# Attention scores in 64x64 tiles of the array, and a cross product's last keys in 32x32 tiles over two banks

## The chip, the core and the metric

One core of a Trainium2 chip runs the whole program in one launch. The metric is the device time of that launch in microseconds. The engines are TensorE (PE in the rows; its weight loads are PEld), VectorE (DVE), ScalarE (ACT), GpSimd (POOL) and SyncE (SP), which issues most DMAs. Each engine works through its own list of instructions in order and waits on semaphores.

## What is computed

Two decoder layers on x of shape (4, 512, 128), with a context of shape (4, 154, 128). The parts that matter here are the first layer's self attention (causal, 16 heads of 8) and its cross attention (16 heads of 8, over 154 context keys):

```python
scores = jnp.einsum('bshd,bthd->bhst', q / jnp.sqrt(Hd).astype(q.dtype), k)
scores = jnp.where(future[None, None, :, :], jnp.finfo(scores.dtype).min, scores)
attn = jax.nn.softmax(scores, axis=-1)
ctx = jnp.einsum('bhst,bthd->bshd', attn, v)
...
scores = jnp.einsum('bhqd,bhkd->bhqk', qh, kh) * scale   # cross: 512 queries, 154 keys
attn = jax.nn.softmax(scores, axis=-1)
out = jnp.einsum('bhqk,bhkd->bhqd', attn, vh)
```

Each is followed by a projection, a residual sum and a layer norm. Then come a gated sum of 8 experts, a linear attention, a second cross attention over the same context with 8 heads, and a gated feed-forward. These five are called "the rest" below.

## The kernel before

**Units.** The self and cross attention of the first layer are done in 32 turns, one for each batch, kind (a = 0 self, a = 1 cross) and group g of four heads. Queries and keys stand in Q6 and K6 as 64 rows for a head (8 features in bf16 parts, and rows that carry the negative maximum), two heads side by side on the partitions: head r of a pair on partitions 64r to 64r+63. A turn has these steps:

- "S" (`scores`, L1117): queries by keys, only to find each query's maximum. Five units u a self turn (SELF_PIECES: two of one piece and three of two), four a cross turn. A unit takes two banks of PSUM, one for each head r. A matmul has 64 rows and 128 columns of weights (L1129), so two of them, r = 0 and 1, lie side by side in the array. In self units the causal mask is added by matmuls of `ident2` with `maskS` (L1136): over 64 columns of each piece (e = 1), then over 128 (e = 0).
- VectorE reduces each unit to maxima (`maxima`, L1820, L1832 to L1837). TensorE transposes them (`max_T`, "mT"), ScalarE copies them, and a DMA on SyncE's queue puts them into Q6 (L804).
- "ST" (`scores_T`, L1141): keys by queries, with the maxima in. Again five self units, of the same widths, with `maskT` (L1158, L1165). A cross turn has two units of 512 queries for the first 128 keys, and one (u = 2) for the last 26 keys, padded to 32, of all four heads in one bank: four matmuls of 64 rows and 32 columns (L1149). ScalarE takes the exponential of each unit into EX (L1570).
- "PV" (`values`, L1170): values by exponentials in f32. A matmul in f32 stands as two records in the trace. Self: 16 matmuls in 128x32 tiles (L1192). Cross: four in 128x32 tiles over 512 queries for the first 128 keys (L1179), then one of the whole array, 128x128 (L1182), for the last keys of the four heads: its weights VXR are block-diagonal, with head j on rows 32j and columns 32j. All into one bank.
- "PV_out": ScalarE copies the bank to `pvraw` (L1474). "cT": TensorE transposes it, and VectorE divides by the sums.

Setup: GpSimd builds `ident2` (L881), the masks and VXR's zeros and ones (L903, L905), and clears Q6[1] in one instruction once the setup products ("wM") are done (L1005). VectorE writes VXR for each batch in `cross_v` (L1918). "wT" are 14 setup transposes of context and weights.

**Order.** It is written out: MERGE is a string of 951 letters, each of which takes the next group of steps from one of 16 streams (`merged`, L363). It sets the order on every engine. BANK_OF names the PSUM bank of each step that fills one; `in_pair` says which steps take the next bank too. A step waits until the earlier users of its banks are drained (`fill`, L1042). Turn (0, self, 0) comes first, then the turns of ORDER; the steps of the rest lie between those of later batches' turns, and the last batch's rest stands alone at the end.

## Time and profile before

| | us |
|---|---|
| median of 3 runs | 489.23 (486.65 to 489.41) |
| the profiled execution | 487.79, of which the span is 486.0 |
| TensorE busy | 459.1 (94%) |
| VectorE busy | 378.0 (78%) |
| ScalarE busy | 344.3 (71%) |
| GpSimd busy | 187.5 (39%) |
| mean granted clock of TensorE | 0.985 of full speed |

A matmul's record runs from its start to its modelled end and overlaps the next one, so the time that a matmul takes from TensorE is read from the distance between starts, not from its own length. In the timeline rows, neighbouring matmuls of one line and form are put together: the first start, the time to the last end, and the count.

### The profile page before, as it was taken

The numbers are of one execution on the slowest core, as the hardware profiler recorded it, in microseconds if no ns is written. First come the engines' busy times: TensorE is split into PE (matmuls) and PEld (weight loads), VectorE is DVE, ScalarE is ACT, GpSimd is POOL, SyncE is SP. The second block draws the span as 40 slices with busy tenths as digits, with TensorE's granted clock in tenths as the row PEclk, the third lists the DMA queues.
The fourth block names the chain that finished last, engine by engine and source line by source line (L and its number), as shares of the span: only waits on it lengthen the run. The fifth ranks groups of instructions, "written<-read, shape, count | busy, mean of one in ns | idle before, by whom it ended". The sixth has DMA issues, their size and how long they took to land.

```text
span 486.0 us, 11581 instructions
## 1 busy us (share of the span) xinstructions
PE 459.1 (94%) x4048; PEld 304.6 (63%) x4048; DVE 378.0 (78%) x1083; ACT 344.3 (71%) x879; POOL 187.5 (39%) x349
## 2 busy tenths in 40 slices
PE   6687899999999999999999999999999999999995
PEld 4454557655455556666777565567764756896895
DVE  4489888798898999995798888847878678765557
ACT  3535758877868788877757787985776868958742
POOL 8590002650204452533233331433414536835423
PEclk9589999999999999999999999999999999999999
DMA  7851300033210211200003000030000000000001
GB/s 229 189 131 36 100 5 25 13 100 82 58 24 1 67 39 35 69 2 0 4 16 93 9 3 2 3 81 13 3 12 14 0 1 2 1 1 1 2 1 43
DMA packets 27181, 18.34 MB, mean 38 GB/s; under 512 B 8217, under 2 KB 26773, under 8 KB 26997
## 3 DMA queue, kind: packets, MB, share of 16 engines
q1 hardware_dynamic: 23413, 15.44, 12.0%
q10 hardware_dynamic: 3712, 2.17, 1.8%
q8 instruction: 33, 0.54, 0.5%
q14 instruction: 23, 0.19, 0.1%
HBM read 5.58 MB, written 1.05 MB: 14 GB/s over the span
## 4 chain that ended last, share of the span: by engine, by line
PE 38%; POOL 5%; DVE 4%; ACT 3%; issue 3%; SPq 1%; DMA 1%; POOLq 0%; DVEq 0%; ACTq 0%
PE psum L1066 5%; PE psum L1425 4%; PE psum L1436 4%; PE psum L1402 3%; PE psum L1338 3%; PE psum L1129 2%; PE psum L1158 2%; PE psum L1192 2%; PE psum L1182 2%; PE psum L1179 2%; SPq L797 1%; PE psum L1447 1%; POOL GP L1024 1%; POOL rstd_rest L955 1%; ACT REST L1653 1%
## 5 line engine op out<-in xcount | busy, mean ns | idle before, releaser
L1570 ACT ACTIVATE EX<-psum 128x1024 f32<-128x1024 f32 (+1 forms) x128 | 118.1, 979 | 12.9 <-PE psum L1165 8.3
L1837 DVE TENSOR_REDUCE mparts<-psum 128x2 f32<-128x768 f32 (+1 forms) x96 | 77.5, 861 | 4.8 <-PE psum L1136 4.5
L1832 DVE TENSOR_REDUCE mparts<-psum 128x4 f32<-128x616 f32 (+1 forms) x80 | 67.8, 875 | 4.7 <-PE psum L1129 4.0
L1129 PE MATMUL psum<-K,Q 64*128 64x154 bf16 (+4 forms) x512 | 47.4, 268 | 5.6 <-issue 2.1
L1024 POOL TENSOR_TENSOR GP<-REST,xrs 128x512 f32<-128x512 f32 (+1 forms) x48 | 33.1, 713 | 46.6 <-DVE xrs L2066 32.6
L1158 PE MATMUL psum<-Q,K 64*128 64x512 bf16 (+3 forms) x320 | 41.4, 315 | 3.6 <-DMA Q<-mrows 1.8
L1653 ACT ACTIVATE REST<-psum,nxmax 128x154 f32<-128x154 f32 x96 | 36.2, 396 | 10.1 <-DVE nxmax L2056 7.9
L1474 ACT COPY pvraw<-psum 128x512 f32<-128x512 f32 x32 | 18.7, 584 | 32.4 <-PE psum L1192 23.4
L1192 PE MATMUL psum<-EX,V 128*32 128x256 f32 (+3 forms) x512 | 37.7, 435 | 0.0
L1129 PEld LDWEIGHTS psum<-K,Q 64*128 64x128 bf16 x512 | 19.0, 95 | 28.9 <-issue 18.4
L952 POOL TENSOR_SCALAR rstd_rest<-moments_rest 128x2 f32<-128x2 f32 x32 | 7.3, 228 | 74.9 <-DVE moments_rest L1872 74.4
L952 POOL TENSOR_SCALAR rstd_attn<-moments_attn 128x4 f32<-128x4 f32 x8 | 1.9, 238 | 83.9 <-DVE moments_attn L1872 83.8
L2056 DVE TENSOR_REDUCE nxmax<-psum 128x2 f32<-128x308 f32 x64 | 28.8, 469 | 5.6 <-PE psum L1402 5.2
L1402 PE MATMUL psum<-GP,xT 128*128 128x308 f32 x96 | 30.5, 433 | 0.1
L1192 PEld LDWEIGHTS psum<-EX,V 128*32 128x32 f32 x512 | 14.6, 109 | 18.4 <-issue 16.9
L1136 PE MATMUL psum<-maskS,ident 64*128 64x128 bf16 (+2 forms) x320 | 24.7, 232 | 0.0
L1698 ACT ACTIVATE X<-Y_rest,shift_rest,rstd_rest 128x128 f32<-128x128 f32 x36 | 15.9, 493 | 11.8 <-POOL shift_rest L960 11.7
L1425 PE MATMUL psum<-VM,REST 128*128 128x128 f32 x192 | 23.8, 277 | 0.2 <-DVE VX L1928 0.2
L955 POOL TENSOR_TENSOR rstd_rest<-rstd_rest,power 128x2 f32<-128x2 f32 x32 | 22.9, 716 | 2.7
L1165 PE MATMUL psum<-maskT,ident 64*128 64x128 bf16 (+2 forms) x320 | 23.8, 227 | 0.0
L1425 PEld LDWEIGHTS psum<-VM,REST 128*128 128x128 f32 x192 | 22.6, 192 | 1.3 <-issue 0.7
L1158 PEld LDWEIGHTS psum<-Q,K 64*128 64x128 bf16 x320 | 13.0, 94 | 15.9 <-issue 6.8
(343 smaller groups left out, 1150.2 us busy)
## 6 DMA issues: line engine op xcount, KB each, us to landing
Q<-xparts SPq DMA_DIRECT2D x24, 128.0 KB
Q<-parts SPq DMA_DIRECT2D x21, 128.0 KB
K<-parts SPq DMA_DIRECT2D x21, 128.0 KB
X<-in_x SPq DMA_DIRECT2D x4, 256.0 KB, 3.1
Q<-in_L_xattn_Wkv SPq DMA_DIRECT2D x1, 1024.0 KB, 7.2
K<-xkparts SPq DMA_DIRECT2D x24, 38.5 KB
out<-XB_rest SPq DMA_DIRECT2D x6, 128.0 KB, 1.8
Q<-in_L_xattn_Wq SPq DMA_DIRECT2D x1, 512.0 KB, 4.3
```

The costliest lines, as they stand in the source:

```text
L955: return nc.gpsimd.tensor_tensor(to, to, half_power, ALU.pow)
L1024: last = nc.gpsimd.tensor_tensor(of.XP[:, at:at + 4 * n].rearrange("p (h c) -> p h c", h=4)[:, :, 0:c1 - c0], of.XE[:, :, c0:c1], of.xrs.r ...
L1129: last = mm(to[:, r, at:at + n], Q6[a][p, b % 2, 2 * g + jj, P * q:P * q + P], K6[a][p, b % 2, 2 * g + jj, 0:n], start=at == 0 or bool(a), ...
L1158: last = mm(to[:, r, at:at + n], K6[a][p, b % 2, 2 * g + jj, P * k:P * k + P], Q6[a][p, b % 2, 2 * g + jj, P * k:S], start=at == 0 or bool ...
L1192: last = mm(to[32 * h:32 * h + 32, P * k:S], V[:, k, 4 * g + h, :], EX[:, ex_slot(b, a, g, u) + h % 2, at:at + n], start=k == PV_ORDER[0], ...
L1402: fills_(mm(fill(key)[:, 0:2 * C], half_of(b, h).xT[4][:, P * q:P * q + P], G[:, head:head + 2, :].rearrange("p h c -> p (h c)")), key)
L1425: mm(to, of.XPT[:, head, :], VM[:, head, :], start=head == 0, stop=False)
L1570: drains(nc.scalar.activation(dst, src, ACT.Exp), key)
L1653: last = nc.scalar.activation(of.XE[:, i, :], src[:, C * j:C * j + C], ACT.Exp, bias=of.nxmax[:, i:i + 1], accum_out=of.xsum[:, i:i + 1])
L1832: last = vec.tensor_reduce(nmax[:, :, :, q], src[:, :, 0:2 * n].rearrange("p r (j k) -> p r j k", j=2), AX.X, ALU.max, negate=True)
L1837: last = vec.tensor_reduce(nmax[:, :, jj, q], src[:, :, at:at + P * (q + 1)], AX.X, ALU.max, negate=True)
L2056: vec.tensor_reduce(of.nxmax[:, 2 * side:2 * side + 2], src, AX.X, ALU.max, negate=True).then_inc(xmax_ready[z], 1)
```

## The change

- **S and ST in 64x64 tiles.** Each matmul of 64 rows and 128 columns becomes two of 64 rows and 64 columns, e = 0 and 1, which write partitions 0 to 63 and 64 to 127 of the same bank. In self units the half e that needs fewer keys (S) or queries (ST) gets 64 fewer. The mask is four matmuls a unit as before, but each has 64 rows of output: S adds 128 columns of mask to half 0 and 64 to half 1; ST 64 and 128. `ident2` shrinks to 64 columns. Matmuls of L1129 and L1158 double, from 512 to 1024 and from 320 to 640.
- **The last cross keys.** ST's unit u = 2 becomes eight matmuls of 256 queries: in the second half of the queries, head h stands on partitions of head h + 2 (modulo 4). PV for cross takes a pair of banks, one for each half of the queries: eight matmuls in 128x32 tiles over 256 queries each, then eight in 32x32 tiles, with rows 32h in the first half and 32(h + 2) in the second. VXR holds every head's 32 columns at all four row groups, so `cross_v` writes 128 columns in each of its four parts instead of 32. ScalarE copies the two half banks in one instruction.
- **The clear** of Q6[1] on GpSimd is eight memsets of 512 words, the last of which signals.
- **New tables** MERGE and BANK_OF of the same lengths; MERGE has each letter as often as before.

What the tables say, when they are followed step by step: in both, turn (0, cross, 0) begins at about the 172nd of 1031 steps and turn (3, cross, 0) at the 692nd. Before the first S unit, the old one has one "wT" (n = 0) and the new one nine (n = 0 to 8), four of them ahead of "qkT". Counted over TensorE's order, neighbouring pieces of work differ in the shape of their tiles 265 times with the old tables and tiles, and 302 times with the new. Of the 16 cross PV steps, 12 are followed in the old order by work of the whole array. In the core of the diff, the rows of the tables after the first are left out:

```diff
--- before.py
+++ after.py
@@ -327,36 +327,38 @@
-    return step[1] in ("S", "ST") and not (step[1] == "ST" and step[2] and step[4] == 2)
+    _, what, *at = step
+    return (what == "S" or what == "ST" and not (at[0] and at[2] == 2)
+            or what == "PV" and at[0] == 1)
...
 MERGE = (
-    "rrrrrrrrlwrrlllwrrrurrsssssuuuvuuuuussssstttrsrttslssspptssttttpsslsrppsttststtupllu"
...
+    "rrrrrruuuurrlrwrlllwuururrrruusssssvusrsssttsstrltstsslspptssttttpsssrplptststtstplu"
...
 BANK_OF = (
-    "024613570246124602454675401724062402640724062460240672460246042604523605260426402367"
...
+    "714325431736704126510425310562402642050362406246024067246702640260452604260426402367"
@@ -464,7 +466,7 @@
-            zeros = VXR[CR:32, :, :].rearrange("p g c -> p (g c)").bitcast(BF16)
+            zeros = VXR[CR:32, :, :].rearrange("p h c -> p (h c)").bitcast(BF16)
             return (Q6[a][MAX_ROWS, b % 2, :, :].rearrange("p (o j) t -> p o (j t)", o=4),
@@ -494,7 +496,7 @@
-        ident2 = sb("ident2", [P, 2, P], BF16)
+        ident2 = sb("ident2", [P, TILE], BF16)
         maskS = sb("maskS", [P, 2, P], BF16)
@@ -541,7 +543,7 @@
         VX = sb("VX", [P, H, 32])
-        VXR = sb("VXR", [P, NQ, P])
+        VXR = sb("VXR", [P, H, 32])
         mparts = sb("mparts", [P, 2, 80])
@@ -878,8 +880,8 @@
                 p = slice(TILE * r, TILE * r + TILE)
-                nc.gpsimd.affine_select(out=ident2[p, :, :], in_=ones_of[p, :, :],
-                                        pattern=[[TILE, 2], [-1, P]], compare_op=ALU.is_equal,
+                nc.gpsimd.affine_select(out=ident2[p, :], in_=ones_of[p, 0, 0:TILE],
+                                        pattern=[[-1, TILE]], compare_op=ALU.is_equal,
                                         fill=0.0, base=0, channel_multiplier=1)
@@ -903,7 +905,7 @@
                     step(nc.gpsimd.memset(
-                        VXR[32 * j:32 * j + CR, :, 32 * j + HD:32 * j + HD + 1], 1.0))
+                        VXR[32 * j:32 * j + CR, :, HD:HD + 1], 1.0))
                 nc.gpsimd.memset(vaug[:, :, :], 1.0).then_inc(late_zeros_ready, 1)
@@ -1002,8 +1004,10 @@
                     pool.wait_ge(bank_filled[k], m + 1)
-                    nc.gpsimd.memset(words(Q6[1].rearrange("p b h t -> p (b h) t")), 0.0
-                                     ).then_inc(cross_rows_ready, 1)
+                    zeroed = words(Q6[1].rearrange("p b h t -> p (b h) t"))
+                    for i in range(8):
+                        last = nc.gpsimd.memset(zeroed[:, S * i:S * i + S], 0.0)
+                    last.then_inc(cross_rows_ready, 1)
                     step(nc.gpsimd.memset(XP, 0.0))
@@ -1114,6 +1118,22 @@
+            def in_tiles():
+
+                for e in R:
+                    for r in R:
+                        yield e, r, *[slice(TILE * i, TILE * i + TILE) for i in (e, r)]
+
+            def mask(to, starts, of, cols_of):
+
+                for e, r, half, p in in_tiles():
+                    cols = cols_of[e]
+                    last = mm(diagonals(to[half, r, :], starts, cols), ident2[p, :],
+                              of[p, e:e + 1, cols].to_broadcast(
+                                  [TILE, len(starts), cols.stop - cols.start]),
+                              start=False, stop=True, skip_group_check=True)
+                return last
+
             def scores(b, a, g, u):
@@ -1123,19 +1143,16 @@
                 for at, jj, q in PIECES[a][u]:
-                    n = C if a else P * (q + 1)
-                    for r in R:
-                        p = slice(TILE * r, TILE * r + TILE)
-                        last = mm(to[:, r, at:at + n], Q6[a][p, b % 2, 2 * g + jj, P * q:P * q + P],
-                                  K6[a][p, b % 2, 2 * g + jj, 0:n], start=at == 0 or bool(a), stop=bool(a))
-                for e in (() if a else (1, 0)):
-
-                    cols = slice(TILE * e, P)
-                    for r in R:
-                        p = slice(TILE * r, TILE * r + TILE)
-                        last = mm(diagonals(to[:, r, :], [at + P * q for at, _, q in PIECES[a][u]], cols),
-                                  ident2[p, e, :], maskS[p, e:e + 1, cols].to_broadcast([TILE, len(PIECES[a][u]), cols.stop - cols.start]),
-                                  start=False, stop=e == 0)
+                    for e, r, half, p in in_tiles():
+
+                        n = C if a else P * q + TILE * (e + 1)
+                        last = mm(to[half, r, at:at + n],
+                                  Q6[a][p, b % 2, 2 * g + jj, P * q + TILE * e:P * q + TILE * e + TILE],
+                                  K6[a][p, b % 2, 2 * g + jj, 0:n], start=bool(a) or at == 0,
+                                  stop=bool(a), skip_group_check=not a)
+                if not a:
+                    last = mask(to, [at + P * q for at, _, q in PIECES[0][u]], maskS,
+                                [slice(0, P), slice(TILE, P)])
                 fills_(last, key)
@@ -1144,28 +1161,33 @@
                 if a and u == 2:
-                    for h in range(4):
+                    for n, h, rest, cols in rests():
                         p = slice(TILE * (h % 2), TILE * (h % 2) + TILE)
-                        last = mm(to[32 * h:32 * h + 32, :], K6[1][p, b % 2, 2 * g + h // 2, P:CP],
-                                  Q6[1][p, b % 2, 2 * g + h // 2, :], start=True, stop=True)
+                        last = mm(to[rest, cols], K6[1][p, b % 2, 2 * g + h // 2, P:CP],
+                                  Q6[1][p, b % 2, 2 * g + h // 2, cols], start=True, stop=True,
+                                  skip_group_check=True)
                     fills_(last, key)
...
                 for at, jj, k in ([(0, u, 0)] if a else SELF_T_PIECES[u]):
-                    n = S - P * k
-                    for r in R:
-                        p = slice(TILE * r, TILE * r + TILE)
-                        last = mm(to[:, r, at:at + n], K6[a][p, b % 2, 2 * g + jj, P * k:P * k + P],
-                                  Q6[a][p, b % 2, 2 * g + jj, P * k:S], start=at == 0 or bool(a), stop=bool(a))
-                for e in (() if a else R):
-
-                    cols = slice(0, TILE * e + TILE)
-                    for r in R:
-                        p = slice(TILE * r, TILE * r + TILE)
-                        last = mm(diagonals(to[:, r, :], [at for at, _, _ in SELF_T_PIECES[u]], cols),
-                                  ident2[p, e, :], maskT[p, e:e + 1, cols].to_broadcast([TILE, len(SELF_T_PIECES[u]), cols.stop - cols.start]),
-                                  start=False, stop=e == 1)
+                    for e, r, half, p in in_tiles():
+
+                        q = P * k + (0 if a else TILE * e)
+                        last = mm(to[half, r, at + q - P * k:at + S - P * k],
+                                  K6[a][p, b % 2, 2 * g + jj, P * k + TILE * e:P * k + TILE * e + TILE],
+                                  Q6[a][p, b % 2, 2 * g + jj, q:S], start=at == 0, stop=bool(a),
+                                  skip_group_check=not a)
+                if not a:
+                    last = mask(to, [at for at, _, _ in SELF_T_PIECES[u]], maskT,
+                                [slice(0, TILE), slice(0, P)])
                 fills_(last, key)
+
+            def rests():
+
+                for n in HALVES:
+                    for h in range(4):
+                        at = 32 * ((h + 2 * n) % 4)
+                        yield n, h, slice(at, at + 32), slice(HS * n, HS * n + HS)
@@ -1175,12 +1197,17 @@
                         drained(pe, (b, "xv"))
-                    for h in range(4):
-                        mm(to[32 * h:32 * h + 32, :], VX[:, 4 * g + h, :],
-                           EX[:, ex_slot(b, a, g, h // 2) + h % 2, :],
-                           start=True, stop=False, skip_group_check=True)
-                    fills_(mm(to, VXR[:, g, :], EX[:, ex_slot(b, a, g, 2), :], start=False, stop=True,
-                              skip_group_check=True), key)
+                    to = pair(key)
+                    for n in HALVES:
+                        for h in range(4):
+                            mm(to[32 * h:32 * h + 32, n, 0:HS], VX[:, 4 * g + h, :],
+                               EX[:, ex_slot(b, a, g, h // 2) + h % 2, HS * n:HS * n + HS],
+                               start=True, stop=False, skip_group_check=True)
+                    for n, h, rest, cols in rests():
+                        last = mm(to[32 * h:32 * h + 32, n, 0:HS], VXR[rest, 4 * g + h, :],
+                                  EX[rest, ex_slot(b, a, g, 2), cols], start=False, stop=True,
+                                  skip_group_check=True)
+                    fills_(last, key)
                     return
@@ -1476,6 +1503,9 @@
+            def halved(t):
+                return t.rearrange("p (n t) -> p n t", n=2)
+
             def place_first(b, y, w):
@@ -1577,6 +1607,12 @@
                 drains(copy(mrows[:, parity(b, a, g), :], src[0:48, 0:64].bitcast(BF16)), key)
+
+            def products_out(b, a, g):
+                key = (b, "PV", a, g)
+                filled(act, key)
+                drains(copy(halved(pvraw[:, :]), pair(key)[:, :, 0:HS]) if a else
+                       copy(pvraw[:, :], bank(key)), key)
@@ -1706,7 +1742,7 @@
                     "ST": exponentials, "mT": max_T,
-                    "PV_out": lambda b, a, g: move(pvraw[:, :], (b, "PV", a, g)),
+                    "PV_out": products_out,
                     "ctxT": lambda b, a: move(ctxT[:, :], (b, "ctxT", a)),
@@ -1921,10 +1957,8 @@
                     vec.tensor_tensor(
-                        VXR[at, :, 32 * j:32 * j + HD],
-                        src[at, P:2 * P].rearrange("p (g h d) -> p g h d", g=NQ, h=4)[:, :, j, :],
-                        rows[at, BV, :].rearrange("p (g h d) -> p g h d", g=NQ, h=4)[:, :, j, :],
-                        ALU.add)
+                        VXR[at, :, 0:HD], src[at, P:2 * P].rearrange("p (h d) -> p h d", d=HD),
+                        rows[at, BV, :].rearrange("p (h d) -> p h d", d=HD), ALU.add)
                 drains(vec.tensor_tensor(VX[:, :, 0:HD],
...
```

## Rows read from the trace of the kernel before

**Rows 1.** Stretches: length, busy (count) of PE, PEld, DVE, ACT, POOL; clock, DMA

```profile
0.00:60.00 60.00, 45.06 (x425) 28.69 (x426) 42.70 (x101) 29.92 (x50) 28.22 (x49) 0.89 0.51 136
...
60.00:220.00 160.00, 156.60 (x1643) 93.22 (x1641) 142.21 (x364) 123.45 (x255) 52.46 (x86) 1.00 0.16 40
...
220.00:380.00 160.00, 158.74 (x1345) 103.28 (x1344) 124.16 (x370) 119.42 (x314) 55.73 (x116) 1.00 0.08 19
...
380.00:486.00 106.00, 98.66 (x642) 79.41 (x640) 68.93 (x250) 71.54 (x262) 51.14 (x99) 0.99 0.02 6
...
27.00:60.00 33.00, 28.90 (x375) 17.72 (x376) 30.47 (x49) 19.33 (x30) 9.13 (x13) 0.95 0.30 80
```

**Rows 2.** Timeline, matmuls of three self units: start, us, form, count

```profile
158.21 0.39 PE L1129 MATMUL psum<-K,Q 64*128 64x512 bf16 x2
...
158.52 0.38 PE L1129 MATMUL psum<-K,Q 64*128 64x512 bf16 x2
...
158.91 0.65 PE L1307 MATMUL psum<-mv,cT 128*32 128x128 f32 x16
...
139.55 0.39 PE L1129 MATMUL psum<-K,Q 64*128 64x256 bf16 x4
...
139.94 0.38 PE L1158 MATMUL psum<-Q,K 64*128 64x512 bf16 x2
...
140.16 0.25 PE L1165 MATMUL psum<-maskT,ident 64*128 64x64 bf16 x4
```

**Rows 3.** Timeline, a cross unit, a cross product and what follows it

```profile
202.95 0.31 PE L1129 MATMUL psum<-K,Q 64*128 64x154 bf16 x4
...
203.19 1.06 PE L1179 MATMUL psum<-EX,VX 128*32 128x512 f32 x8
...
204.18 1.13 PE L1182 MATMUL psum<-EX,VXR 128*128 128x512 f32 x2
...
205.15 0.60 PE L1066 MATMUL psum<-ident,X 128*128 128x128 f32 x4
```

**Rows 4.** Timeline, another cross product, followed by a score unit

```profile
138.49 1.13 PE L1182 MATMUL psum<-EX,VXR 128*128 128x512 f32 x2
```

**Rows 5.** Groups by line and form: count, busy us, mean ns

```profile
L1149 PE MATMUL psum<-Q,K 64*32 64x512 bf16 x64 | 6.3, 387 | 0.0
...
L1129 PEld LDWEIGHTS psum<-K,Q 64*128 64x128 bf16 x512 | 19.0, 95 | 28.9 <-issue 18.4 <-ACT EX L1570 2.9 <-DMA Q<-xparts 1.7
...
L1192 PEld LDWEIGHTS psum<-EX,V 128*32 128x32 f32 x512 | 14.6, 109 | 18.4 <-issue 16.9 <-ACT EX L1570 0.9
...
L1182 PEld LDWEIGHTS psum<-EX,VXR 128*128 128x128 f32 x32 | 4.8, 188 | 13.4 <-issue 13.4
...
L1201 PEld LDWEIGHTS psum<-identb,mparts 128*80 128x80 bf16 x32 | 3.7, 117 | 2.4 <-issue 2.0
```

**Rows 6.** Stretches again, for L1136 alone, then for L1182 alone

```profile
60.00:220.00 160.00, 12.73 (x172) 7.71 (x172) 1.00 0.16 40
...
220.00:380.00 160.00, 5.13 (x68) 3.05 (x68) 1.00 0.08 19
...
60.00:220.00 160.00, 6.75 (x12) 1.78 (x12) 1.00 0.16 40
```

**Rows 7.** Waits: us in total, times, longest us

```profile
ACT pvraw L1474 <- PE psum L1182: 9.0, 7, 2.6
```

**Rows 8.** Timeline of the start, with the setup transposes

```profile
14.85 1.97 PE L1066 MATMUL psum<-ident,qkn 128*128 128x128 f32 x8 [5.37 <-DVE qkn L1770]
...
27.10 0.39 PE L1129 MATMUL psum<-K,Q 64*128 64x512 bf16 x2 [2.08 <-issue]
...
32.53 1.64 PE L1066 MATMUL psum<-ident,Q 128*128 128x128 f32 x13
```

**Rows 9.** Groups by line: two memsets of GpSimd

```profile
L1005 POOL MEMSET Q<- 128x4096 f32 x1 | 3.5, 3512 | 4.4 <-PE psum L1253 4.4
...
L903 POOL MEMSET VXR<- 128x512 f32 x1 | 0.5, 524 | 0.1
```

40 lines of the change are left out of this document (20 added, 20 removed).

## The prediction

> **What bounds the kernel now.** I read the busy time by stretches first. From 60 to 380 us TensorE is busy 98 to 99% of the time, VectorE 89% up to 220 us and 78% after it, and the granted clock is 1.00, the 2.4 GHz level [rows 1]. But a busy TensorE may be one that waits with overlapping records, so I read the timeline next, by distances between starts. A self unit of S with one piece takes 158.52 - 158.21 = 0.31 us. Its two matmuls side by side have 512 columns, its masks 64 and 128: 704 columns at 2.4 GHz are 0.293 us, and four steps of some 3 ns make it 0.31. A unit with two pieces (256 + 256, masks of 128 and 256: 896 columns, 0.373 us) takes 139.94 - 139.55 = 0.39 us, and 512 columns alone take 140.16 - 139.94 = 0.22 us [rows 2]. So in such runs TensorE is bound by the columns that stream through it: columns that are taken away there are time. The same one-piece unit, followed by work in another shape of tiles, takes 158.91 - 158.52 = 0.39 us: a change of shape costs 0.08 to 0.09 us [rows 2]. The start is another matter: from 27 to 60 us VectorE is busy 30.5 of 33 us and TensorE 28.9 [rows 1]. After 380 us there is only the rest, where TensorE is busy 98.7 of 106 us [rows 1] and which the change does not touch.
>
> **Self units in four tiles.** With the halves e side by side, a one-piece unit streams 448 + 128 columns in one half and 512 + 64 in the other: 576 / 2.4 = 0.240 us, with the steps 0.25. A two-piece unit streams at most 640: 0.267 us, with the steps 0.28. ST is the mirror image. Against 0.31 and 0.39 that saves 0.06 and 0.11 us. Matmuls start in the order of the list, so one half sometimes waits for the other; I take 0.01 off each. A turn has two and three such units in S, and again in ST: 2 x 0.05 + 3 x 0.10 = 0.40 us a side, and 32 sides make 12.8 us.
>
> **Does the array do it?** No row shows 64x64 tiles. The nearest is 64x32: 64 matmuls of 387 ns are busy 6.3 us, that is 0.39 us for each four, so four tiles in two row groups run at once, each with its own stream [rows 5]. In 128x32 tiles, 16 matmuls of 128 columns in f32 take 0.65 us [rows 2], four at a time. From above: if halves ran at once at no cost, 12.8 us plus the 1.6 that I took off. From below: one after the other, which is a rival below. I take the near end.
>
> **Weight loads.** A load of 64x128 in bf16 takes 95 ns, one of 80 columns 117 ns; in f32, 32 columns take 109 ns and 128 take 188 ns, 0.82 ns a column [rows 5]. A load starts when the tile's previous matmul starts, so only its streaming part can hold the next one. At 0.82 ns, 64 columns take 53 ns, as long as a mask of 128 columns streams; only a mask of 64 columns (27 ns) is shorter. So the cost lies between nothing and 0.026 us x 160 units = 4.2 us. I take nothing: the extra 22 ns of the 80-column load over the 128-column one is less than what a mask of 64 columns streams. The Trainium skill speaks against the change here ("TensorEngine Tiling (Array Packing)", Restrictions and Gotchas): column tiling switches off the fast weight load, which the 64x128 loads have and the 64x64 ones would not. By that rule the sum would be up to 4.2 us worse; the trace agrees so far that the 80-column bf16 load is the longer one.
>
> **Cross units.** S: four matmuls of 154 columns two at a time become eight, four at a time: the same 0.13 us of streaming (a unit takes 203.19 - 202.95 = 0.24 us with the change of shape [rows 3]), and 0.01 us for the longer row of starts, 64 times: -0.6 us. ST's units of 512 queries stay at 0.22 us; the last keys' eight matmuls of 256 columns are two on each of four tiles, as long as four of 512: nothing.
>
> **Cross products.** The first part takes 204.18 - 203.19 = 0.99 us [rows 3]; four rounds of 256 columns for two of 512 leave it. The second takes 205.15 - 204.18 = 0.97 us where work of the whole array follows [rows 3], and 139.55 - 138.49 = 1.06 us where a score unit does [rows 4, 2]. Its two records are 2 x 512 / 1.2 = 0.853 us (f32 streams at half rate), the rest is the first weight load. After: eight tiles, all different, so two records of 256 columns: 0.427 us; a load of 32 columns for 128, 0.03; eight starts, 0.05; a change of shape behind it, always, 0.09: 0.60 us. Twelve products save 0.37 and four 0.46: 6.3 us. If the two halves ran one after the other it would be 16 x 0.43 = 6.9 us less, none; I take the near end, as eight tiles share nothing. ScalarE copies the same 512 columns as before.
>
> **New tables.** Changes of shape go from 265 to 302. Twelve of these 37 are in the products' 0.60; the other 25 cost 25 x 0.09 = 2.3 us. Eight more setup transposes come ahead of the first score. TensorE idles 5.4 us before 14.85 and 2.1 before 27.10, and five of the eight show later as 13 records in 1.64 us and more of the kind [rows 8]; nothing is lost by them if their loads have landed, and what they free lies in 27 to 60 us, where VectorE is the bound. Bounds: 0 and some 6 us (eight at up to 0.87 us, the time of eight records 0.11 us apart).
>
> **Other edits.** `cross_v` writes wider pieces on VectorE, a few tenths of a us over four batches. The clear: 4096 words take 3.5 us, 512 take 0.52, so eight take at most 4.2 [rows 9]; 0.7 us more on GpSimd, busy 52 of 160 us there [rows 1], hides under the work of TensorE; without that cover it would be 0.7 us. A smaller `ident2` is ahead of the scores by 20 us: nothing.
>
> **The sum.** 12.8 + 6.3 - 0.6 - 2.3 = 16.2 us of TensorE. Where do they fall? Of 320 mask matmuls in S, 172 run in 60 to 220 us and 68 after, which leaves 80 before 60 us; of the 32 records of the whole-array product 12 run in 60 to 220 us [rows 6].
> - To 60 us: 3.2 us of self units. VectorE leaves 33 - 30.5 = 2.5 us; I take 2.0, with whatever the moved transposes give.
> - 60 to 220 us: 6.9 + 2.4 - 1.6 (costs by share) = 7.7 us. VectorE would then be busy 142.2 of 152.3 us, 93%, and each engine waits for the others through eight banks. I take two thirds: 5.1.
> - 220 to 380 us: 2.7 + 3.9 - 1.3 = 5.3 us, with VectorE at 124 of 155: all of it.
> - After 380 us: nothing.
>
> Together 12.4 us. The profiled execution took 487.8 us, 1.8 outside its span; 487.8 - 12.4 = 475.4. The median stands 1.4 us higher, which gives 476.8. I take 476.
>
> **Rivals.**
> 1. *Starts come no closer than they do now.* The densest run in the rows is 15 starts in 0.65 - 0.28 = 0.37 us, 25 ns each [rows 2]. If that is a floor, a cross unit of eight needs 0.20 us and not 0.13 (64 x 0.065 = 4.2 us) and a two-piece unit of twelve 0.30 and not 0.28 (96 x 0.02 = 1.9). 482 us. For it: no denser run; against: neighbours in one round start a few ns apart. The skill's "TensorE: Matmul & The Clock Gate" (Wait — 56ns, not 53.3ns?) has such a floor, about 25 ns from start to start however few the columns; the starts inside a round are closer than it says. Chance 12%.
> 2. *VectorE becomes the bound* up to 220 us. Only the last stretch gains, 5.3 us: 484 us. For it: 89 and 92% busy; against: TensorE was 98% busy beside it. 16%.
> 3. *Weight loads bind* by 4.2 us: 480 us. 4%.
> 4. *Slower: the pair for cross products.* They need two neighbouring banks free where one did, while score units take pairs too, and all that TensorE has behind them (score units that VectorE and ScalarE wait for) waits along. ScalarE waited up to 2.6 us for such a product [rows 7], so delays of this size exist. Each us that one product waits costs 16; above 12.4 / 16 = 0.78 us each the gain is gone. At 1.1 us it is 494 us. Against: the order was written anew with the pairs in it. 10%, of which 4% stay within 1%.
> 5. *Slower: halves do not run at once.* One-piece units would take 0.48 us, two-piece 0.53, and the cross ones 0.13 and 0.21 more: 32 x (2 x 0.17 + 3 x 0.14) + 64 x 0.13 + 32 x 0.21 = 39 us, less 6.3: about 522 us. It costs more than it gains when less than about two thirds of the halves overlap. 6%.
>
> **Numbers.** The forecast has 52%. About 1%, 5 us, is what a measurement of this kernel can tell from no change. Faster by more: 52 + 12 + 4 + 7 of rival 2 = 75%. Within: 9 of rival 2 and 4 of rival 4, 13%. Slower: 12%. The range: down to 489 - 16.2 - 6 = 467 if all of TensorE's gain and all of the moved transposes count, up to 486, past rivals 1 to 3. The forecast's own range is 469 to 481.
>
> **What would show it.** Distances between starts of units: 0.25 and 0.28 us for self units, about 0.60 us from the first 32x32 matmul to the next work; cross units at 0.13 us before the change of shape. TensorE's busy time some 12 to 15 us lower, at an unchanged tail of about 106 us; VectorE above 91% from 60 us on. It is wrong if units take 0.30 us and more, if TensorE shows idle time ahead of the cross products, or if VectorE waits longer than before for S units.

## The result, and the profile after

The changed kernel takes 484.94 us (median of 20 runs, 484.05 to 488.91), the kernel before 487.78 us beside it (20 runs, 486.53 to 490.68): a ratio of 0.994, 95% interval 0.9924 to 0.9956. It is faster by 2.8 us, 0.6%, within the 1% that I called no change; I had forecast 12 us. The profiled execution has a span of 484.8 us against 486.0.

The stretches of the changed kernel, in the columns of [rows 1], show that the matmuls were not what failed:

```profile
27.00:60.00 33.00, 27.48 (x477) 15.31 (x481) 31.08 (x53) 19.07 (x27) 9.62 (x12) 0.80 0.31 80
60.00:220.00 160.00, 152.17 (x2203) 90.20 (x2193) 143.79 (x357) 120.22 (x245) 53.21 (x95) 0.98 0.16 42
...
220.00:380.00 160.00, 158.67 (x1922) 105.99 (x1922) 128.39 (x380) 123.21 (x325) 55.13 (x116) 1.00 0.07 18
```

From 60 to 220 us TensorE is busy 152.2 us where it was 156.6, and VectorE 143.8 against 142.2: TensorE has got idle time, and VectorE is hardly busier for it. The granted clock, 1.00 there before, is 0.98, and from 27 to 60 us 0.80 in place of 0.95.

The timeline of the changed kernel (start, us, form, count) answers to [rows 2 to 4]: S units at 133.90 (one piece) and 136.20 (two), a cross product at 134.61 and 135.61, an ST unit of two pieces at 141.48.

```profile
133.90 0.41 PE L1149 MATMUL psum<-K,Q 64*64 64x448 bf16 x4
...
134.16 0.34 PE L1149 MATMUL psum<-K,Q 64*64 64x320 bf16 x6
...
134.61 1.07 PE L1203 MATMUL psum<-EX,VX 128*32 128x256 f32 x16
135.61 0.66 PE L1207 MATMUL psum<-EX,VXR 32*32 32x256 f32 x16
136.20 0.36 PE L1149 MATMUL psum<-K,Q 64*64 64x320 bf16 x6
...
136.50 0.38 PE L1176 MATMUL psum<-Q,K 64*64 64x512 bf16 x4
...
141.48 0.38 PE L1176 MATMUL psum<-Q,K 64*64 64x128 bf16 x8
...
141.76 0.38 PE L1176 MATMUL psum<-Q,K 64*64 64x128 bf16 x8
```

From start to start: one piece 134.16 - 133.90 = 0.26 us (0.31 before), two pieces 136.50 - 136.20 = 0.30 and 141.76 - 141.48 = 0.28 us (0.39 before), the first part of the product 1.00 us (0.99), the second 136.20 - 135.61 = 0.59 us (0.97 to 1.06). Not every unit saves as much. The medians of all self units of ST after 60 us are 0.27 us (one piece) and 0.30 us (two) where another score unit follows, for 0.31 and 0.39 before; where the shape of the tiles changes behind them they are 0.37 and 0.40 us, for 0.40 and 0.49.

Where the time went can be read off one instruction of VectorE that ends the maxima of each of the 32 turns. Timelines, six of the 32, the kernel before and then the changed one:

```profile
59.76 0.17 DVE L1847 TENSOR_TENSOR mparts<-mparts 128x16 f32<-128x16 f32 x1
...
102.98 0.17 DVE L1847 TENSOR_TENSOR mparts<-mparts 128x16 f32<-128x16 f32 x1
...
152.88 0.17 DVE L1847 TENSOR_TENSOR mparts<-mparts 128x16 f32<-128x16 f32 x1
...
181.84 0.17 DVE L1847 TENSOR_TENSOR mparts<-mparts 128x16 f32<-128x16 f32 x1
...
225.21 0.17 DVE L1847 TENSOR_TENSOR mparts<-mparts 128x16 f32<-128x16 f32 x1
...
366.37 0.17 DVE L1847 TENSOR_TENSOR mparts<-mparts 128x16 f32<-128x16 f32 x1
```

```profile
58.90 0.17 DVE L1883 TENSOR_TENSOR mparts<-mparts 128x16 f32<-128x16 f32 x1
...
100.19 0.17 DVE L1883 TENSOR_TENSOR mparts<-mparts 128x16 f32<-128x16 f32 x1
...
150.22 0.17 DVE L1883 TENSOR_TENSOR mparts<-mparts 128x16 f32<-128x16 f32 x1
...
183.30 0.28 DVE L1883 TENSOR_TENSOR mparts<-mparts 128x16 f32<-128x16 f32 x1
...
227.13 0.17 DVE L1883 TENSOR_TENSOR mparts<-mparts 128x16 f32<-128x16 f32 x1
...
365.09 0.18 DVE L1883 TENSOR_TENSOR mparts<-mparts 128x16 f32<-128x16 f32 x1
```

The changed kernel is 0.9 us ahead at 59 us, 2.8 at 100, 2.7 at 150; then 1.5 us behind at 182 and 1.9 at 225; and 1.3 ahead at 366, and 1.2 at the end. So there are two things to explain: 4.2 us lost at one place between 150 and 183 us, and gains that are small everywhere else.

To size them I added up TensorE's records. A record streams its columns at 2.4 GHz (512 columns of bf16 in 0.22 us) or, in f32, at 1.2 GHz (256 columns in 0.215 us, the distance of two rounds in the product at 134.61). The rest is half clock (what the same columns take longer while the granted clock is at its 1.2 GHz level), changes of shape (idle time where the shape changes, up to 93 ns each) and waits:

```
us                         waits   streaming  half clock  changes (count)
before                      50.2     396.4       7.9       25.9 (284)
tiles alone, old tables     57.7     385.7      10.4       25.9
tables alone                52.6     396.9       8.1       28.0 (306)
changed                     56.4     380.2      14.0       28.6 (315)
changed, addition held      55.6     380.2      10.8       28.6
held, both readers light    50.0     380.6       6.5       28.6
```

16.2 us of streaming are gone and 2.7 us of changes of shape have come, 13.5 us net; 6.2 us came back as waits and 6.1 us as stretches at 1.2 GHz. The other rows are from runs below. The rows leave out some 5.6 us of the span, and how overlapping records are divided between the columns is a choice: another division moves a column by up to 6 us, but the differences between the rows by no more than 0.6.

### The profile page after: what moved, and what is told of

The parts are those of the page before. It is cut to its first block, busy times and chain, and to the rows that moved or that the text cites. A ratio compares the mean times of both kernels' runs of the same rounds, so it can differ in the third digit from the quotient of the medians.

```text
span 484.8 us, 14106 instructions
## 1 busy us (share of the span) xinstructions
PE 454.0 (94%) x5296; PEld 304.7 (63%) x5296; DVE 383.4 (79%) x1083; ACT 346.0 (71%) x879; POOL 187.7 (39%) x356
## 4 chain that ended last, share of the span: by engine, by line
PE 72%; DVE 11%; ACT 5%; SPq 4%; issue 3%; POOL 2%; DMA 2%; POOLq 0%; DVEq 0%; ACTq 0%
PE psum L1070 10%; PE psum L1452 6%; PE psum L1219 6%; PE psum L1429 6%; PE psum L1365 6%; PE psum L1149 5%; DVE mparts L1873 4%; PE psum L1176 4%; PE psum L1463 4%; PE psum L1203 3%; PE psum L1474 2%; SPq L771 2%; PE psum L1207 2%; DMA K<-parts 2%; PE psum L1247 2%
## 5 line engine op out<-in xcount | busy, mean ns | idle before, releaser
L1149 PE MATMUL psum<-K,Q 64*64 64x154 bf16 (+8 forms) x1024 | 51.2, 274 | 8.4 <-DVE mparts L1873 2.7
L1176 PE MATMUL psum<-Q,K 64*64 64x512 bf16 (+7 forms) x640 | 43.3, 320 | 3.2 <-ACT EX L1600 1.1
L1149 PEld LDWEIGHTS psum<-K,Q 64*64 64x64 bf16 x1024 | 22.7, 108 | 34.5 <-issue 15.7
L1176 PEld LDWEIGHTS psum<-Q,K 64*64 64x64 bf16 x640 | 16.2, 108 | 19.6 <-issue 7.7
L1365 PE MATMUL psum<-ew,xT 128*128 128x512 f32 x48 | 24.8, 656 | 0.0
L1615 ACT COPY pvraw<-psum 128x512 f32<-128x512 f32 x16 | 9.4, 584 | 20.5 <-PE psum L1219 20.5
L1131 PE MATMUL psum<-maskS,ident 64*64 64x128 bf16 (+2 forms) x320 | 22.3, 241 | 0.0
L933 POOL COPY V<-qkn 128x256 f32<-128x256 f32 x8 | 3.7, 467 | 44.8 <-PE psum L1219 44.7
```

Source lines behind the costliest of these rows:

```text
L1149: last = mm(to[half, r, at:at + n], Q6[a][p, b % 2, 2 * g + jj, P * q + TILE * e:P * q + TILE * e + TILE], K6[a][p, b % 2, 2 * g + jj, 0:n ...
L1176: last = mm(to[half, r, at + q - P * k:at + S - P * k], K6[a][p, b % 2, 2 * g + jj, P * k + TILE * e:P * k + TILE * e + TILE], Q6[a][p, b ...
L1365: fills_(mm(fill(key), half_of(b, h).xT[2][:, P * i:P * i + P], ew[:, 4 * side:4 * side + 4, :].rearrange("p e d -> p (e d)")), key)
```

## Experiments

Each was timed beside the kernel before; the number given is the ratio to it with its 95% interval. A difference of two such ratios is uncertain by 1.6 to 2.1 us.

### The parts one by one

**Tiles alone, old tables.** The kernel before with the score units in 64x64 tiles and nothing else:

```diff
...
-                        last = mm(to[:, r, at:at + n], Q6[a][p, b % 2, 2 * g + jj, P * q:P * q + P],
...
+                    for e, r, half, p in in_tiles():
...
+                        last = mm(to[half, r, at:at + n],
+                                  Q6[a][p, b % 2, 2 * g + jj, P * q + TILE * e:P * q + TILE * e + TILE],
...
```

> The kernel before with its own MERGE and BANK_OF, its own cross product and its one-piece clear; only the score units S and ST run in 64x64 tiles. By the sum, TensorE streams some 12 us less. Theory A (the array was the bound only in part: what it is spared comes back as waits for VectorE and ScalarE and as stretches at the 1.2 GHz level, whatever the order): about 4 to 5 us faster than before, ratio about 0.991, with more wait and more half-clock time in the trace. Theory B (the new tables bring the waits and the clock drops): 9 to 11 us faster, ratio about 0.98, and faster than the changed kernel, with the clock as high as in before.

**Tables alone.** The new `MERGE` and `BANK_OF` with the pair of banks for the cross product and the clear in eight pieces; the score tiles and the product are those of before, and ST's last keys run as eight matmuls of 256 queries in place of four of 512:

> The new MERGE and BANK_OF (the cross product holds two banks and fills one) and the eight-piece clear, with the score tiles and the cross product of before. Streamed columns as before. Theory A: within 2 us of before. Theory B: 5 to 9 us slower than before, with drops of the clock after 27 us that before does not have.

**Tiles on the new tables**, with the product of before:

> The changed kernel with the cross product of before (VXR block-diagonal, one 128x128 matmul for the last keys, one bank filled of the two held). Against the changed kernel TensorE streams 6.3 us more. Theory A: 2 to 4 us slower than the changed kernel, about level with before. Theory B: the product is full profit wherever it stands, so 6 us slower than the changed kernel, some 3 us slower than before. If the pair of banks were what costs (rival 4), this kernel would have the same waits ahead of the products and not be slower by more than its 6 us of streaming.

**Product on the new tables**, with the score units of before:

> The changed kernel with the 64x128 score tiles of before. Against the changed kernel TensorE streams some 12 us more. Theory A: 3 to 6 us slower than the changed kernel, so level with or up to 3 us slower than before, with less wait and less time at the lower clock than the changed kernel. Theory B: 10 us or more slower than the changed kernel, about 1.5% slower than before.

Measured: tiles on the old tables 0.9972 (0.995 to 0.9994), tables alone 1.0089 (1.0064 to 1.0114), tiles on the new tables 1.0027 (1.0006 to 1.0049), product on them 1.0001 (0.998 to 1.0023). So the new tables cost 4.3 us by themselves; on them the tiles are worth 3.0 us and the product 4.3, and both together 7.3 (1.0089 to 0.994): they add up. On the old tables the tiles are worth 1.4 us, although the sum of records gives 10.7 us less streaming. What is missing there is no cost of the tiles themselves but something that takes the gain. The eight-piece clear is in all kernels with the new tables and was not timed by itself.

### Is it VectorE? Is it the clock at the start?

**Fewer columns for the maxima**, for the kernel before and for it with the tiles (`[:, :, :, 0:n // 2]` on what the two kinds of `tensor_reduce` read; these kernels leave out half of the keys in the maxima and serve for the time alone):

> The kernel before, but VectorE's maxima of the first layer's scores read the first half of each piece's keys only, so some 60 to 70 us of VectorE's 378 us are gone; TensorE's work is unchanged. The maxima are then not those of all keys. If TensorE alone bounded the kernel: within 1 us of before. If VectorE sets the pace up to 220 us (rival 2 of the prediction): 3 to 6 us faster than before.

> The same lighter maxima with the 64x64 score tiles and the old tables (e1). What the tiles are worth with VectorE out of the way is this kernel against e6. Theory of rival 2 (VectorE took the gain): 8 to 11 us faster than e6. Theory E (the gain is lost elsewhere: ScalarE's exponentials, latencies from engine to engine, the clock): 1 to 3 us faster than e6, as e1 is against before.

Measured: 0.9955 (0.9933 to 0.9978) without the tiles and 0.9954 (0.9924 to 0.9984) with them. With VectorE light the tiles are worth nothing on the old tables (0.0 us, give or take 1.8), so VectorE alone is not what takes the gain there. Idle time of TensorE's weight loads for S from 60 to 380 us, without and with tiles (after the bar: busy; idle, and what ended it):

```profile
L1129 PEld LDWEIGHTS psum<-K,Q 64*128 64x128 bf16 x446 | 15.7, 94 | 21.9 <-issue 15.0 <-ACT EX L1570 2.1 <-DMA Q<-xparts 1.1
```

```profile
L1145 PEld LDWEIGHTS psum<-K,Q 64*64 64x64 bf16 x896 | 18.6, 106 | 28.1 <-issue 15.8 <-DMA K<-parts 3.2 <-ACT EX L1580 3.1
```

With tiles there are twice as many loads and the idle time before them is 6.2 us longer; no VectorE is among its first releasers: ScalarE's exponentials (1.0 us more) and a transfer of keys (3.2) are.

**Dummy matmuls at the start**, four ahead of each of the first ten S units, to hold the clock up:

> The kernel with 64x64 score tiles and the old tables (e1), with four matmuls of 128 columns in f32 (about 0.9 us at 2.4 GHz) put ahead of each of the ten S units of the first batch's first two turns, into the unit's own bank; they compute nothing that is kept. In e1 the clock stood at 1.2 GHz until 37.8 us (30.9 in before) and the second turn's scores were done 2.7 us later than in before. Theory C (the low clock at the start costs e1 its gain): the clock is up by about 31 us, the second turn's scores are done at about 42 us, and the kernel is 2 us faster than e1, ratio about 0.993 to before. Theory D (VectorE sets the pace there, and the clock is a symptom): no faster than e1, 0 to 3 us slower.

Measured: 1.0154 (1.0121 to 1.0186). From 27 to 60 us the granted clock was 0.95 instead of 0.84, and yet the second turn's maxima ended at 50.84 us instead of 44.35. The dummies took more of TensorE than the clock gave back. That does not say which engine bounds the start without them, for with them VectorE is busy only 22.7 of the 33 us. The runs with light maxima say more. The stretch from 27 to 60 us, tiles on the old tables, then the same with light maxima:

```profile
27.00:60.00 33.00, 27.86 (x467) 17.42 (x467) 28.25 (x46) 18.41 (x28) 9.12 (x12) 0.84 0.26 69
```

```profile
27.00:60.00 33.00, 26.56 (x491) 16.90 (x491) 21.10 (x54) 20.71 (x32) 9.17 (x12) 0.95 0.30 78
```

With less for VectorE to read, the clock is at 0.95 with no dummy at all, and the instruction that ends the fourth turn's maxima starts at 57.57 us instead of 61.74. In the kernel before it starts at 57.25 with light maxima and at 59.76 without. So VectorE does hold up the start, as I had it in the prediction; what I had left out is that TensorE's clock goes down with it.

### Both readers of the score banks

A score unit needs two banks, and they are free once VectorE (maxima) or ScalarE (exponentials) has read them. If that sets the pace, the tiles pay when both read less. Beside the light maxima, ScalarE's exponentials leave out half of each bank from the second batch on:

```diff
...
+                elif b:
+                    dst, src = EX[:, slot_:slot_ + 2, 0:S // 2], pair(key)[:, :, 0:S // 2]
                 else:
                     dst, src = flat(EX[:, slot_:slot_ + 2, :]), flat(pair(key))
...
```

> The kernel before with two kinds of work cut in half: both of VectorE's kinds of row maxima read half of their columns (as in the run of the kernel before with light maxima), and from the second batch on ScalarE's exponentials of a two-bank unit read and write only the first 256 of 512 columns of each bank. The rest of EX keeps older numbers, so this is a kernel for the time alone, and the reference point of the next run. Both theories: somewhat faster than with light maxima alone (485.69 us), where PE's waits that ScalarE's exponentials end were 6.2 us between 40 and 240 us; 476 to 485 us.

> The same two cuts, with the score units in 64x64 tiles and the tables of before; it differs from the run before it in the tiles alone. With the full load of the two engines the tiles were worth 1.4 us of 11 us of matmul time saved, with the light maxima nothing (PE's waits for ScalarE's exponentials grew from 6.2 to 9.1 us). Theory of the banks (a unit that is done sooner waits for the two banks of the next one, which VectorE or ScalarE must first have read): with both readers light the gain appears, 5 to 9 us below the run before it. Rival (the gain goes into something other than the readers of the banks: transfers, the clock after waits, the order's waits of SyncE's table): still within 2 us of it.

Measured: 0.9993 (0.9963 to 1.0023) without the tiles and 0.9879 (0.9845 to 0.9913) with them. The kernel before gains nothing from two light readers (I had expected some us), and its streaming and its waits stay as they were within 0.3 us: its TensorE is the bound. The 2.2 us that light maxima alone gave it are not seen here; in this profile it is 3.4 us ahead at 60 us, but the granted clock falls for 3.4 us at 106 us, and at 366 us it is 1.1 ahead. Between the two kernels with light readers the tiles are worth 5.6 us (1.14%) by these ratios, 6.9 us by the medians, where they were worth 1.4 with full readers. So the tiles' gain is there, and it is the load on the two readers that withholds it.

### The order and the banks

**Everything in the old order of work**, with a table of banks that I worked out from the times of before, and again with a better one:

> The changed kernel (tiles, two-bank product, eight-piece clear) with the old MERGE, and a bank table laid out anew from the fill and drain times of the trace of before. If the new tables cost what e2 shows (4 us against before) and the parts add up: before - 1.4 (tiles) - 4.3 (product) = 482.5 us, ratio about 0.988, 2 us faster than the changed kernel. If the new order only costs where the old work runs in it: level with the changed kernel, 0.994.

> All of the change's matmuls and copies with the order of work of before, as the run of this kind that took 520 us, but with another table of banks, which leaves 48 of the steps less than 100 ns between the last read of their bank and their first matmul (by the times of before), where that one left 172, and the kernel before leaves 38. Theory of the banks: the 35 us that the other one cost were waits for banks that its table made; with this table it is 478 to 490 us, and it tells whether the new order is worth anything beside a fitting table of banks. Rival (the product's pair of banks can't be had in the old order, whatever the table): over 495 us.

> The product of the cross keys as in the change (two banks, 32x32 tiles over halves of the queries), with the score units of before, the order of work of before and the table of banks of the run with everything in the old order (487.31 us). Theory: the product saves 6.3 us of matmul time and costs 23 more shape changes at 0.09 us and waits for its second bank; on the new tables it was worth 4.3 us. If the waits for banks set the time, the tiles are worth under 2 us here too, and it is 485 to 489 us. Rival (the tiles carry the gain in the old order once banks fit): 490 to 493 us.

Measured: 1.0663 (1.0636 to 1.0691), then 0.9998 (0.9976 to 1.002), and the product alone in the old order 1.0000 (0.9976 to 1.0024). Both kernels of everything issue the same matmuls in the same order; only `BANK_OF` differs, and 32 us hang on it. In the first, TensorE was idle in the middle:

```profile
60.00:220.00 160.00, 142.89 (x2187) 84.29 (x2178) 135.36 (x347) 117.53 (x223) 50.32 (x89) 1.00 0.17 43
...
220.00:380.00 160.00, 146.03 (x1764) 97.86 (x1762) 116.75 (x325) 112.81 (x307) 50.38 (x102) 1.00 0.07 18
```

The granted clock is 1.00 and nobody is busier: these are waits for banks. With the better table the whole change is worth nothing in the old order, 2.8 us less than with the new tables. So the new tables are worth having with the new matmuls, though they cost 4.3 us with the old ones. Order and banks are not separated by this: my better table leaves 48 steps less than 100 ns between the last read of their bank and their first matmul, where the kernel before has 38, and a better one still might give the old order more.

### The loss between 150 and 183 us

The timeline of the changed kernel there, start and duration first:

```profile
160.96 1.41 DVE L1978 TENSOR_TENSOR gl<-gl,gs 128x16 f32<-128x16 f32 x1
161.08 1.26 POOL L947 TENSOR_TENSOR XB_attn<-X,rows 128x512 f32<-128x512 f32 x1
...
162.30 1.28 DVE L1873 TENSOR_REDUCE mparts<-psum 128x2 f32<-128x768 f32 x2
...
163.63 0.64 PE L1149 MATMUL psum<-K,Q 64*64 64x192 bf16 x8 [1.44 <-DVE mparts L1873]
...
165.37 5.90 PE L1365 MATMUL psum<-ew,xT 128*128 128x512 f32 x8
```

and its stretches:

```profile
162.00:166.00 4.00, 2.56 (x45) 1.92 (x38) 3.76 (x13) 3.08 (x5) 0.34 (x1) 0.63 0.00 0
166.00:170.00 4.00, 4.00 (x6) 1.55 (x5) 2.30 (x7) 1.65 (x4) 0.00 (x0) 0.52 0.00 0
```

A small subtraction on VectorE takes 1.41 us, eight times its usual 0.17, and ends when GpSimd's addition ends (162.37 and 162.34 us). The maxima behind it are late, TensorE waits 1.44 us for them, and from 163.0 us, during this wait, the granted clock is at its 1.2 GHz level, so that eight expert matmuls take 5.90 us. In the kernel before, this addition ran at 150.34 us, while VectorE read PSUM for its maxima. It is the new tables that bring the two together: in the kernel with the tables alone the subtraction takes 0.98 us, at 164.78.

**The addition in four pieces:**

```diff
...
-                nc.gpsimd.tensor_tensor(
-                    XB_attn[:, :, :], X1[:, :, :],
-                    rows[:, BO:BO + 1, :].to_broadcast([P, NB, D]), ALU.add
-                ).then_inc(residual_ready, 1)
+                for n in range(NB):
+                    last = nc.gpsimd.tensor_tensor(XB_attn[:, n, :], X1[:, n, :], rows[:, BO, :], ALU.add)
+                last.then_inc(residual_ready, 1)
...
```

> The changed kernel with one thing changed: GpSimd's addition of rows to all four blocks of X1 (XB_attn, one instruction of 1.26 us at 161 us) is issued as four instructions of a quarter each. Theory: in the changed kernel VectorE's small instruction beside it took 1.41 us in place of 0.17 us, TensorE waited 1.5 us for what stood behind it, and the granted clock then fell for 7 us; with pieces the small instruction waits for a quarter at the most, the wait is under 0.8 us, the clock stays up at 163 us, and the time is 1.5 to 4 us below the changed kernel's (481 to 483.5 us). Rival: the contention is the same in sum, or the gain ends in the next wait, and the time is that of the changed kernel within 1 us (484 to 486 us).

Measured: 0.9988 (0.9964 to 1.0011), 2.3 us slower than the changed kernel's 0.994. My theory of a short wait fell: VectorE did not get in between the pieces.

```profile
161.96 1.84 DVE L1977 TENSOR_TENSOR gl<-gl,gs 128x16 f32<-128x16 f32 x1
162.08 1.69 POOL L948 TENSOR_TENSOR XB_attn<-X,rows 128x128 f32<-128x128 f32 x4
...
165.05 0.64 PE L1148 MATMUL psum<-K,Q 64*64 64x192 bf16 x8 [1.86 <-DVE mparts L1872]
```

The subtraction took 1.84 us, until all four were done. The Trainium skill ("SBUF — State Buffer", SBUF: two separate sides) describes such a stall: VectorE and GpSimd share a pair of ports under an exclusive lock, when VectorE's instruction has two inputs in SBUF and GpSimd's reads SBUF, and whoever starts first has it for the whole instruction. The trace agrees on the stall, and with the tables alone, where the addition starts first (164.47 us), on who loses. Here the one that starts first by the records (by 0.12 us) is the one that loses, and it loses to four instructions in a row. That the ports are the cause no run here shows by itself; that the meeting of the two instructions is, the next one does.

**The addition held back** until the subtraction is done:

```diff
...
                 pool.wait_ge(x_ready[1], b + 1)
+                if b == 1:
+                    pool.wait_ge(gate_shifted[1], 1)
...
```

> The changed kernel with one wait more: before its addition of rows to X1 (XB_attn) in the second batch, GpSimd waits until VectorE's small subtraction on the gates' logits (gl, line 1978) is done, so that the two don't meet. The addition then runs beside VectorE's maxima, which read PSUM. Theory (VectorE's instruction is held until all of GpSimd's work on the queue is done, TensorE waits for the maxima behind it, and the granted clock then falls): the small instruction takes 0.17 us as elsewhere, TensorE's wait at 163.6 us is under 0.6 us, the clock stays at its full level there, and the time is 2 to 4.5 us below the changed kernel's (480.5 to 483 us). Rival: the clock falls at 163 us for another reason, or the gain ends in the next wait, and it stays within 1 us of the changed kernel (484 to 486 us).

> The changed kernel itself, profiled and timed once more beside the others. Theory: its granted clock falls at the same places as in its first profile, because the waits ahead of them come from the order of work: at 163 us and at 391 us within 1 us, and the time is 484 to 486 us. Rival (the falls are chance of one execution): at other places, or none.

Measured: held 0.9885 (0.9854 to 0.9915), 482.42 us; the changed kernel again 0.9931 (0.9904 to 0.9958), 484.63 us. The timeline of the kernel with the held addition:

```profile
162.60 0.17 DVE L1980 TENSOR_TENSOR gl<-gl,gs 128x16 f32<-128x16 f32 x1
...
162.95 1.26 POOL L949 TENSOR_TENSOR XB_attn<-X,rows 128x512 f32<-128x512 f32 x1 [0.25 <-DVE gl L1980]
...
164.03 0.41 PE L1151 MATMUL psum<-K,Q 64*64 64x192 bf16 x8 [0.20 <-DVE mparts L1875]
...
180.71 0.28 DVE L1885 TENSOR_TENSOR mparts<-mparts 128x16 f32<-128x16 f32 x1
...
362.65 0.18 DVE L1885 TENSOR_TENSOR mparts<-mparts 128x16 f32<-128x16 f32 x1
```

The subtraction takes 0.17 us, TensorE waits 0.20, the clock stays up, and the maxima that ended 1.5 us later than before at 182 us now end 1.1 us sooner. That is worth 2.2 to 2.7 us (against the two timings of the changed kernel; each is uncertain by 1.7 to 2.0). This version beats both kernels. In the repeated profile of the changed kernel the wait was 1.39 us and the clock fell again at 164 us, but came back after 3.4 us where it took 6.8; at 391 us, where it also fell in the first, it now stayed up. And where only the tiles were on the new tables the same wait stood without any fall:

```profile
165.64 0.41 PE L1149 MATMUL psum<-K,Q 64*64 64x192 bf16 x8 [1.44 <-DVE mparts L1867]
...
166.59 3.70 PE L1360 MATMUL psum<-ew,xT 128*128 128x512 f32 x8
```

So the wait makes the fall possible, not certain; it costs up to 5.90 - 3.70 = 2.2 us on these eight matmuls.

### Which reader

The kernel with the held addition, with both readers light, and with each of them light alone:

> The kernel with the held addition, and with the two cuts of the light runs: VectorE's maxima over half of their columns, and from the second batch on ScalarE's exponentials of a two-bank unit over half of theirs. Theory of the banks: tiles, product and tables together save 16.2 us of streaming and cost 2.7 us of shape changes; against the kernel before with both cuts (487.59 us) the time falls by most of that, to 472 to 478 us, where with the full load it fell by 2.8 us. Rival (the new order has slack of its own that isn't the readers'): 479 to 484 us, no further below the run with tiles alone and both cuts (480.71 us) than 2 us.

> The kernel with the held addition (482.42 us) and only ScalarE's exponentials of a two-bank unit cut in half from the second batch on, VectorE's maxima whole; with both cuts it took 473.37 us. If ScalarE is what holds the banks: 473 to 477 us. If VectorE is: 481 to 483 us. If each takes over where the other is light, as the tiles alone showed with light maxima: 478 to 482 us, and the same for the other run.

> The kernel with the held addition (482.42 us) and only VectorE's maxima cut in half, ScalarE's exponentials whole. If VectorE is what holds the banks: 473 to 477 us. If ScalarE is: 481 to 483 us. If each takes over from the other: 478 to 482 us.

Measured: both light 0.9708 (0.9677 to 0.9739), 473.37 us; exponentials alone 0.9839 (0.9809 to 0.987); maxima alone 0.9772 (0.9741 to 0.9803). Against the held kernel's 0.9885 that is 8.6 us for both, 2.2 for ScalarE, 5.5 for VectorE. Against the kernel before with the same light readers, 0.9993, the whole change is worth 14 us, where the sum of records gives 13.5; with light maxima on both sides (0.9772 against 0.9955) it is worth 9.0. The idle time before the weight loads for S from 60 to 380 us, held kernel, then with light maxima, then with both light:

```profile
L1151 PEld LDWEIGHTS psum<-K,Q 64*64 64x64 bf16 x896 | 18.9, 105 | 25.6 <-issue 12.6 <-DVE mparts L1875 2.2 <-DMA Q<-xparts 1.8
```

```profile
L1151 PEld LDWEIGHTS psum<-K,Q 64*64 64x64 bf16 x888 | 18.7, 105 | 25.1 <-issue 14.6 <-ACT EX L1602 3.2 <-DMA Q<-xparts 2.0
```

```profile
L1151 PEld LDWEIGHTS psum<-K,Q 64*64 64x64 bf16 x872 | 18.6, 105 | 23.7 <-issue 14.8 <-DMA Q<-xparts 1.9 <-ACT EX L1604 0.9
```

Light maxima put ScalarE's 3.2 us in place of VectorE's 2.2; only with both light do these waits go. But the three totals differ by 1.9 us only, and the times by 8.6. The rest stands earlier. The stretch from 27 to 60 us, in the same order:

```profile
27.00:60.00 33.00, 28.19 (x459) 15.34 (x460) 29.84 (x47) 17.55 (x24) 9.46 (x12) 0.71 0.31 80
```

```profile
27.00:60.00 33.00, 27.34 (x497) 15.88 (x501) 23.25 (x57) 18.17 (x26) 9.04 (x12) 0.86 0.31 79
```

```profile
27.00:60.00 33.00, 27.31 (x545) 15.48 (x549) 23.18 (x60) 19.55 (x29) 9.06 (x12) 0.95 0.31 81
```

The start of the instruction that ends the maxima, at three of the 32 turns, and the span, all in us:

| kernel | 4th turn | 21st turn | last turn | span |
|---|---|---|---|---|
| before | 59.76 | 225.21 | 366.37 | 486.0 |
| changed | 58.90 | 227.13 | 365.09 | 484.8 |
| changed, again | 59.09 | 225.98 | 363.89 | 481.9 |
| addition held | 60.47 | 224.53 | 362.65 | 480.7 |
| held, light maxima | 56.58 | 220.99 | 358.43 | 476.8 |
| held, light exponentials | 59.45 | 222.35 | 360.11 | 478.1 |
| held, both light | 55.25 | 215.80 | 352.85 | 471.2 |

Light maxima are worth 4.2 us at the last turn, and 3.9 of them are there by the fourth: they speed up the start, where the clock is higher with them. It is no chance of one execution: over all executions the median of the mean granted clock is 0.972 in the held kernel, 0.983 with light maxima and 0.989 with both light. From the fourth turn to the last, light maxima alone save 0.3 us, light exponentials alone 1.5, and both together 4.6. So from 60 us on it is as I had written of one theory, each reader takes over where the other is light; the larger share of VectorE in the times comes from the start. The sum of records says the same of the whole: of the 9.5 us between the held kernel's span and that with both light, 5.6 are waits and 4.3 half clock.

## Why the prediction was wrong, step by step

- **What the array does: right, and a sixth too large.** One-piece units 0.26 us for 0.25, two-piece 0.28 to 0.30 for 0.28, the product's second part 0.59 for 0.60, its first unchanged. The product's 6.3 us came out; of the 12.8 us of the self units the records show 10.7, as the units ahead of a change of shape save less. Net gain of TensorE 13.5 us by the records, for 16.2. Its busy time fell by only 5.1 us (459.1 to 454.0) and not by the 12 to 15 that I had named as the sign, since stretches at the lower clock count as busy.
- **Rivals 1, 3 and 5 are out** by the same rows: starts in a round stand a few ns apart (the four of the unit at 133.90 within 10 ns), and halves run at once. On weight loads, a load of 64x64 takes 105 to 108 ns, one of 64x128 took 94 to 95, so each is dearer; yet the units take their forecast time, and what I weighed at up to 4.2 us is not seen.
- **The new tables: too small.** I had charged 25 changes of shape at 0.09 us, 2.3 us. By the records they cost 2.1 us, which is right; but the tables alone cost 4.3 us, the rest in waits (50.2 to 52.6 us). I had costed a new order by its changes of shape only, and not by what it puts side by side, such as the addition on GpSimd and the subtraction on VectorE, which meet in that kernel too.
- **To 60 us: 2.0 forecast, 0.9 measured.** That VectorE leaves little room was right: light maxima bring this point forward by 2.5 us in the kernel before and by 3.9 in the held one. What I put at nothing was the clock. It is 0.80 for 0.95 here, and takes much of what the shorter matmuls give; with the tiles on the old tables this point even comes 2.0 us later than before (61.74).
- **From 60 to 220 us: the step that failed.** I took two thirds of 7.7 us, 5.1, to come through. Measured from 60 to 225 us it is a loss of 2.8 us (0.9 ahead, then 1.9 behind), so 7.9 us are missing. With the addition held the stretch takes 164.06 us for 165.45 before, a gain of 1.4: the stalled subtraction and the clock after it are 4.2 us of the missing 7.9 by these profiles (2.8 against the repeated profile of the changed kernel, and 2.2 to 2.7 by the timings of the whole). With both readers light as well it takes 160.55, a gain of 4.9 (and 7.6 against the kernel before with the same light readers, which takes 168.19 and has a fall of the clock there). So what was left is the load of the two readers. A busy TensorE beside a VectorE at 89% was read as a TensorE with room above it. The shares didn't show the next limit: TensorE was busy 14.4 us longer than VectorE, twice the 7.7 us that I took away from it, and yet the gain came back as waits.
- **From 220 to 380 us: 5.3 forecast, 3.2 measured** to the last maxima (1.9 behind at 225, 1.3 ahead at 366). VectorE was busy only 78% there and I let all of the gain through.
- **After the last maxima: nothing, and that was luck.** From there to the end it is 119.6 us before and 119.7 after. But the changed kernel's profile has a fall of the clock for 3.4 us at 391 us. In the repeated profile, without the fall, it is 118.0, and 118.1 in the held kernel: the new tables leave 1.5 us less for the end, and the fall took it back.
- **Rival 2, VectorE as the bound, 484 us at 16%, came nearest,** in its number and in its shape, gain only in the late stretch. As a cause it was half right. VectorE's load holds up the start, where I had expected it; from 60 us on, light maxima alone free 0.3 us and only both readers together 4.6. I had set against it that TensorE was 98% busy beside VectorE. That shows who was the bound before, and says nothing of how far the next one is behind. **Rival 4,** waits of the cross products, is not seen with the new tables: the product is worth 4.3 us there. In the old order with my table of banks it is worth nothing (1.0000) for its 6.3 us, and whether waits for its second bank take them was not looked into.
- **The range** of 467 to 486 holds 484.94, at its edge. The 75% for faster by over 1% were too much: the step "TensorE saves 16, so the kernel saves 12" had a rival of its own in every stretch.

What stays open: light readers free the banks sooner and also deliver maxima and exponentials sooner, and no run separates the two. I can't say how many of the waits each transfer adds, nor why the clock at the start rises at 40 us in one execution (changed) and 46 in another of nearly the same work (held).

## What to carry to other kernels

Where three engines share a few buffers, busy shares don't bound what a saving on the busiest is worth. Here 98% and 89% left 14.4 us between the first two in 160 us, and 7.7 us less for the first gave at most 1.4 us while the others had their full load. Make the readers light in an experiment before the writer is made quick: it costs one run and gives the gain's ceiling. Then read that run by stages, for it can also change the clock at the start, which is another gain than the one looked for. After a new order of work, search the timeline for instructions that take many times their usual duration beside another engine; one wait placed rightly was worth nearly as much as the change itself.
